# Score rows turned by TensorE, output products first in a step, ELU by one exponential, sixteen mask tiles

## The reference

```
h = max(layernorm(x), 0)
# layer 0
D = |h_i - h_j|                       for every pair of nodes of a graph
s = leaky(batchnorm(D W1 + b1)) W2    one score for each pair, symmetric in i, j
A = softmax(where(adj > 0, s + b2, -9e15))
y = leaky(batchnorm((A h) Wg + bg))
x = x + [h, y] Wt + bt
# layer 1
h = max(layernorm(x), 0); v = h W
a = softmax over i of where(adj > 0, leaky(v_i a1 + v_j a2), -9e15)
out = x + elu(a v)
```

## Time and profile before

| | us |
|---|---|
| median of 3 runs | 1188.4 (1184.73 to 1188.98) |
| the profiled execution, its time | 1189.32 |
| the profiled execution, its span | 1187.5 |
| busy in the span: PE, DVE, ACT, POOL | 1062.9, 1058.1, 994.8, 541.3 |
| mean granted TensorE clock | 0.965 |

### The profile page before, as it was taken

One profiled execution on the slowest core, in us unless ns is written; L12 is line 12 of the kernel. 1 busy time (PEld: TensorE's weight loads), 2 busy tenths in 40 slices (PEclk: granted clock), 3 DMA queues, 4 the chain that ended last, 5 costly groups with the idle time before them and its releaser, 6 DMA issues.

```text
span 1187.5 us, 17527 instructions
## 1 busy us (share of the span) xinstructions
PE 1062.9 (90%) x6376; PEld 463.2 (39%) x6376; DVE 1058.1 (89%) x1418; ACT 994.8 (84%) x1238; POOL 541.3 (46%) x251
## 2 busy tenths in 40 slices
PE   3889999999999999999999599999999999548997
PEld 1333333333333333333333212333333333338886
DVE  6899999999999999999999787999999999435787
ACT  3879999999999899999999599898988989006987
POOL 6466667666666666666667101111122211261331
PEclk9989999999999999999999799999999999758998
DMA  6324343434343334343434789999999998700222
GB/s 165 131 118 177 143 173 146 178 142 164 156 178 142 160 160 177 142 168 152 178 142 188 299 305 358 366 355 360 349 358 350 347 348 296 191 4 12 71 80 72
DMA packets 118005, 237.52 MB, mean 200 GB/s; under 512 B 17568, under 2 KB 65952, under 8 KB 117920
## 3 DMA queue, kind: packets, MB, share of 16 engines
q1 hardware_dynamic: 116336, 235.70, 54.6%
q10 hardware_dynamic: 1584, 0.69, 0.3%
HBM read 126.52 MB, written 109.84 MB: 199 GB/s over the span
## 4 chain that ended last, share of the span: by engine, by line
PE 45%; DVE 32%; ACT 9%; issue 7%; DMA 3%; POOL 2%; SPq 1%; POOLq 0%; DVEq 0%; ACTq 0%
PE psum L708 18%; DVE store L275 12%; PE psum L718 11%; PE psum L722 8%; DVE plain_st L979 4%; ACT store L610 3%; ACT store L556 3%; DVE store L1058 3%; DMA early<-score_rows 2%; PE psum L821 1%; PE psum L680 1%; PE psum L698 1%; PE psum L778 1%; PE psum L855 1%; POOL store L475 1%
## 5 line engine op out<-in xcount | busy, mean ns | idle before, releaser
L708 PE MATMUL psum<-store,w1tt_sb 128*64 128x512 f32 x1792 | 426.0, 605 | 37.4 <-ACT store L556 19.2
L275 POOL TENSOR_TENSOR store<-h_ext 128x2048 f32<-128x2048 f32 (+1 forms) x96 | 386.5, 4028 | 140.9 <-PE psum L708 137.0
L275 DVE TENSOR_TENSOR store<-psum,h_ext 128x2048 f32<-128x2048 f32 x160 | 364.0, 2275 | 0.9 <-ACT h_ext L526 0.9
L556 ACT ACTIVATE store<-store 128x2048 f32<-128x2048 f32 x160 | 305.1, 1929 | 15.2 <-DVE store L275 10.3
L708 PEld LDWEIGHTS psum<-store,w1tt_sb 128*64 128x64 f32 x1792 | 121.7, 137 | 277.5 <-issue 223.5
L610 ACT ACTIVATE store<-store,st 128x1024 f32<-128x1024 f32 x192 | 225.8, 1242 | 1.4 <-DVE st L1045 1.4
L718 PE MATMUL psum<-store,w_twice 128*64 128x512 f32 x768 | 201.5, 603 | 3.9 <-DVE early L944 3.5
L979 DVE BATCH_NORM_STATS2 plain_st<-store 128x6 f32<-128x512 f32 x256 | 160.6, 678 | 0.6 <-ACT store L568 0.6
L722 PE MATMUL psum<-early 128*64 128x512 bf16 x1152 | 158.0, 381 | 0.0
L275 DVE TENSOR_TENSOR store<-h_ext 128x2048 f32<-128x2048 f32 x64 | 139.1, 2173 | 2.6 <-PE psum L708 2.6
L778 PE MATMUL psum<-store,w_rows 128*32 128x512 f32 x1024 | 131.8, 606 | 5.4 <-ACT store L610 5.4
(11 more groups left out here) (153 smaller groups left out, 1143.4 us busy)
## 6 DMA issues: line engine op xcount, KB each, us to landing
kept_products<-store SPq DMA_DIRECT2D x192, 512.0 KB, 2.7
store<-kept_products SPq DMA_DIRECT2D x192, 512.0 KB, 7.5
early<-score_skew SPq DMA_DIRECT2D x16, 384.0 KB, 6.4
early<-adj SPq DMA_DIRECT2D x16, 256.0 KB, 8.0
early<-adj_t SPq DMA_DIRECT2D x16, 256.0 KB, 3.0
store<-x SPq DMA_DIRECT2D x16, 256.0 KB, 4.8
out<-early SPq DMA_DIRECT2D x16, 256.0 KB, 2.4
score_rows<-early SPq DMA_DIRECT2D x64, 32.0 KB, 3.7
```

Of the source, the lines that this page charges most:

```text
L275: return engine.tensor_tensor(t[:, :, 0:steps, :], nodes.unsqueeze(2).broadcast_to([C, 2, steps, N]), windows(h_ext[:, 2 * c, :], STEP * m ...
L556: nc.scalar.activation(t, t, ACT.Abs).then_inc(abs_ready, 1)
L708: last = nc.tensor.matmul(t[MID * g:MID * g + MID, b, :], w1tt_sb[:, 0:MID], diff[slot][:, g, b * BANK:b * BANK + BANK], start=True, stop= ...
```

## The change

1. **Score rows.** The DRAM buffer `score_rows`, `store_rows`, `load_dist` and `s_dist` are gone. PE turns the four 128x128 pieces of `s_rows` directly at `DIST_T`, now 21 and no longer 32, and DVE sorts them into `s_turn` by four smaller operations in place of one. All steps behind move to: TURN 22, SUM 37, SCORES 39, EXP 43, NORM 45, TURN_P 48, COPY 49, MIX 51, MIX_COPY 52, OUT 55, Y 57; STORE_SKEW 24, LOAD_HALF 30, LOAD_ADJ 22.
2. **The half sum.** `att_sum` is four transposes and no longer eight products; the straight half is added to the mask by a new POOL operation behind `sum_half` (`half_masked`), for which `att_scores` waits.
3. **Plain chunk 7.** In pass 2 `subtract` does all eight distances in one operation (`repeats=True`); the doubled half of distance 64 is dropped later by `last_mask`.
4. **POOL in the tail.** All 16 `x_and_bias` stand behind the last quad's `sum_half`; the loads of `x` are issued 6 and 10.
5. **PE in the last stage.** The list is `outputs(t+1)`, `values(t-5)`, `turn2(t-3)`, `dense(t-4)`, `attend(t-6)`.
6. **ELU.** ACT does one exponential of the attended values from PSUM; DVE does min(exp, 1) + the rest.
7. **Masks.** Each of sixteen masks has its own tile; six are made in pass 2 as before, ten at steps 1 to 10 of the last stage, their loads issued before it.

```diff
-        EVAC, DIST_T, TURN, SUM, SCORES, EXP, NORM, TURN_P, COPY, MIX, MIX_COPY, OUT, Y = \
-            19, 32, 33, 50, 52, 56, 58, 61, 62, 64, 65, 67, 69
-        STORE_ROWS, LOAD_DIST, STORE_SKEW, LOAD_HALF, LOAD_ADJ = 21, 26, 35, 41, 30
-        TAIL = 72
+            19, 21, 22, 37, 39, 43, 45, 48, 49, 51, 52, 55, 57
+        STORE_SKEW, LOAD_HALF, LOAD_ADJ = 24, 30, 22
+        TAIL = 60
...
+                pool.wait_ge(half_summed, j + 1)
+                nc.gpsimd.tensor_tensor(mneg[:, :, :], mneg[:, :, :], s_half[:, :, 0:N], ALU.add).then_inc(half_masked, 1)
...
             for j in range(NQ):
                 mask(j)
-                if j == NQ - 1:
-                    pool.wait_ge(bt_ready, 1)
-                    for q in range(8):
-                        x_and_bias(q)
                 sum_half(j)
-                if 5 <= j < 5 + MRING:
+                if 5 <= j < 5 + MADE:
                     mask_l1(j - 5)
-            for q in range(8, NQ):
+            pool.wait_ge(bt_ready, 1)
+            for q in range(NQ):
                 x_and_bias(q)
...
-                nc.scalar.activation(MIN[j % 2], bank(A_BANK[j % 2]), ACT.Relu, scale=-1.0).then_inc(neg_ready, 1)
-                act.wait_ge(neg_ready, j + 1)
-                nc.scalar.activation(MIN[j % 2], MIN[j % 2], ACT.Exp, scale=-1.0).then_inc(neg_exp, 1)
+                nc.scalar.activation(MIN[j % 2], bank(A_BANK[j % 2]), ACT.Exp).then_inc(neg_exp, 1)
...
             def turn_dist(j):
-                pe.wait_ge(dist_in, 16 * (j + 1))
+                pe.wait_ge(rows_ready, j + 1)
                 at_one(QCH * j + DIST_T)
-                for b in range(QUAD):
-                    last = nc.tensor.transpose(att[1].rearrange("p b n -> p (b n)")[:, DIST * b:DIST * b + DIST],
-                                               s_dist[0:DIST, b, :], ident[0:DIST, 0:DIST])
+                for d in range(4):
+                    last = nc.tensor.transpose(att[1][:, d, :], s_rows[:, N * d:N * d + N], ident[:, :])
...
             for t in range(-1, STEPS):
-                for lag, do in ((TURN2, turn2), (DENSE, dense), (MASKED, values), (ATTEND, attend), (-1, outputs)):
+                for lag, do in ((-1, outputs), (MASKED, values), (TURN2, turn2), (DENSE, dense), (ATTEND, attend)):
...
-                nc.vector.tensor_tensor(s_turn[:, :, :],
-                                        att[1].rearrange("p b n -> p (b n)")[:, 0:QUAD * DIST]
-                                        .rearrange("p (b d) -> p b d", b=QUAD),
-                                        last_mask[:, :].unsqueeze(1).broadcast_to([N, QUAD, DIST]), ALU.mult)\
-                  .then_inc(turn_ready, 1)
+                turned_rows = att[1].rearrange("p d (q m) -> p d q m", q=4)
+                in_order = lambda t: t.rearrange("p (r q d) -> p r q d", r=4, q=4)
+                for b in range(QUAD):
+                    last = nc.vector.tensor_tensor(in_order(s_turn[:, b, :]),
+                                                   turned_rows[:, :, :, 4 * b:4 * b + 4].rearrange("p d q r -> p r q d"),
+                                                   in_order(last_mask[:, :]), ALU.mult)
+                last.then_inc(turn_ready, 1)
...
-                nc.vector.tensor_tensor(OUT_T[j % 4], OUT_T[j % 4], MIN[j % 2], ALU.add).then_inc(out_ready, 1)
+                nc.vector.scalar_tensor_tensor(OUT_T[j % 4], MIN[j % 2], 1.0, OUT_T[j % 4], ALU.min, ALU.add)\
+                  .then_inc(out_ready, 1)
```

More of the change, by code:

```diff
@@ L55 @@
 LEAD_DIFF = 7
-MRING = 6
+MADE = 6
 LEAD_PROD = 3
@@ L209, in two_layers @@
         x_in2 = [sem(f"x_in2_{j}") for j in range(NQ)]
-        adjt_in = [sem(f"adjt_in{q}") for q in range(MRING)]
+        adjt_in = [sem(f"adjt_in{j}") for j in range(NQ)]
         out_stored = [sem(f"out_stored{q}") for q in range(4)]
@@ L264, in own, with subtract @@
             return h_ext[:, 2 * c:2 * c + 2, 0:N]
-        def subtract(engine, c, m, slot, op, nodes):
+        def subtract(engine, c, m, slot, op, nodes, repeats=False):
             t = diff[slot].rearrange("p g (d i) -> p g d i", i=N)
             steps = STEP
-            if m == PER - 1:
+            if m == PER - 1 and not repeats:
                 steps = STEP - 1
@@ L301, in two_layers @@
         OUT_T = [by_graph(late(512 * q, 512)) for q in range(4)]
-        MASK = [by_graph(late(5120 + 512 * q, 512)) for q in range(MRING)]
-        adjt = [by_graph(late(5120 + 512 * q, 512).bitcast(I32)) for q in range(MRING)]
+        spare = plain_st[:, :, :, :].rearrange("p n t s -> p (n t s)")
+        mask_at = [late(5120 + 512 * q, 512) for q in range(MADE)] + \
+            [spare[:, 512 * q:512 * q + 512] for q in range(4)] + [late(at, 512) for at in (2560, 3072, 2048, 3584, 4096, 4608)]
+        MASK = [by_graph(t) for t in mask_at]
+        adjt = [by_graph(t.bitcast(I32)) for t in mask_at]
+        TILE_FREE = (mask_ready, s_masked, exp_done, prob_turned, mixed, out_mm)
         O_BANK, T_BANK, D_BANK, W_BANK, A_BANK = (0, 1), 2, 3, (4, 5), (6, 7)
@@ L378, in load_adjt @@
             def load_adjt(j):
-                if j >= MRING:
-                    sp.wait_ge(den_masked, j - MRING + 1)
-                sp.dma_start(adjt[j % MRING], adj_tn[:, quad(j), :]).then_inc(adjt_in[j % MRING], 16)
+                if MADE <= j < NQ - len(TILE_FREE):
+                    sp.wait_ge(pass2_ready, 1)
+                elif j >= MADE:
+                    sp.wait_ge(TILE_FREE[j - NQ + len(TILE_FREE)], NQ)
+                sp.dma_start(adjt[j], adj_tn[:, quad(j), :]).then_inc(adjt_in[j], 16)
             AHEAD = LRING
@@ L393, in _ @@
                           .then_inc(skew_stored[s], 16)
-                for step, do in ((LOAD_ADJ, load_adj), (STORE_ROWS, store_rows), (LOAD_DIST, load_dist),
-                                 (STORE_SKEW, store_skew), (LOAD_HALF, load_half)):
+                for step, do in ((LOAD_ADJ, load_adj), (STORE_SKEW, store_skew), (LOAD_HALF, load_half)):
                     j = quad_at(n - AHEAD, step)
@@ L398, in _ @@
                         do(j)
-                        if step == LOAD_ADJ and 4 <= j < 4 + MRING:
+                        if step == LOAD_ADJ and 4 <= j < 4 + MADE:
                             load_adjt(j - 4)
                         if j == NQ - 1 and step != LOAD_ADJ:
-                            part = (STORE_ROWS, LOAD_DIST, STORE_SKEW, LOAD_HALF).index(step)
-                            for q in range(4 * part, 4 * part + 4):
+                            for q in range(6) if step == STORE_SKEW else range(6, NQ):
                                 load_x(q)
@@ L408, in store_out @@
                 sp.dma_start(out_n[:, quad(j), :], OUT_T[j % 4]).then_inc(out_stored[j % 4], 16)
+            for j in range(MADE, NQ):
+                load_adjt(j)
             for t in range(STEPS + 1):
-                if MRING <= t + 1 < NQ:
-                    load_adjt(t + 1)
                 if 0 <= t - LAST - 1 < NQ:
@@ L805, in att_sum @@
                 for b in range(QUAD):
-                    nc.tensor.matmul(att[0][:, b, :], ident[:, :], s_half[:, b, 0:N], start=True, stop=False)
-                    last = nc.tensor.matmul(att[0][:, b, :], s_half[:, b, 0:N], ident[:, :], start=False, stop=True)
+                    last = nc.tensor.transpose(att[0][:, b, :], s_half[:, b, 0:N], ident[:, :])
                 last.then_inc(s_sum, 1)
@@ L1053, in again @@
                     dve.wait_ge(prod2_ready, p - 1)
-                subtract(nc.vector, c, m, p % 2, ALU.subtract, own(c)).then_inc(abs2_step, 1)
+                subtract(nc.vector, c, m, p % 2, ALU.subtract, own(c), repeats=True).then_inc(abs2_step, 1)
                 dve.wait_ge(abs2_step, p + 1)
@@ L1171, in masked @@
                 for b in range(QUAD):
[L1172 removed]
+                    last = nc.vector.tensor_tensor_reduce(DEN[j % 4][:, b, :], DEN[j % 4][:, b, :], MASK[j][:, b, :],
                                                           -1.0, 3e38, ALU.add, ALU.min, soft[:, j % 4, 0, b:b + 1])
```

39 lines of the change are left out of this document (12 added, 27 removed).

## The result

The changed kernel takes 1216.93 us (median of 4 runs, 1216.54 to 1217.86); beside it the kernel before took 1188.69 (median of 4 runs, 1184.73 to 1195.84). The ratio is 1.0241, with a 95% interval of 1.0212 to 1.0269. The forecast of 1196.4 had the sign right and the size wrong: +28 us where +8 stood, and outside the range.

A forecast was written before the change was run, and what follows sets the result against it. DVE was taken to bound pass 2, and in the last stage PE's attend waiting for DVE's chain, which starts after outputs. Pass 2 +8, tail -16, last stage +16 made +8 on 1188.4: 1196.4 us, range 1183 to 1208.

The forecast's parts named there:

- The loop of the last stage: Last stage: outputs first in PE's list closes a PE-ACT loop, steps 8.09 us against 6.63; stage +16 us (+12 to +18).
- The shorter ELU: Last stage: eight ELUs at the end, each one ACT operation shorter, give -4.5 us; inside the loop it is hidden.
- The clock: Rival, last stage: PE's clock falls in the loop's 2.3 us gaps, 3 to 13 us, taken as 5 (1201); chance 0.17.
- the 2.76 of the row: Last stage, kernel before: a PE gap of 2.76 us ended at the lower clock level, at the turn2 at 1081.02.
- Pass 2: Pass 2, bound by DVE: +0.7 us per quad (0.1 to 1.7) for 12 quads, +8 us (+2 to +14).
- POOL's new addition costs DVE something where they meet: Pass 2: one meeting in two quads, +0.2 us per quad (0 to 0.41), from a subtraction taking 2.42 against 2.01.
- The rest of pass 2: Pass 2, per quad: four sorting operations in place of one, +0.25 us; DVE's wait for PE's turned rows, 0.2 us.
- Chunk 7: Pass 2: one full subtraction in place of memset and two subtractions, +0.02 us, twice, counted as nothing.
- The start of attention: Pass 2: attention starting 13 chunks earlier costs about what the waits for score_rows had cost; counted as nothing.
- The tail: From the last scores' end to the last stage: shorter chain, then POOL's 16 x_and_bias late next; -16 us (-12 to -18).
- Sum: Whole kernel: pass 2 +8, tail -16, last stage +16, together +8 us on 1188.4, giving 1196.4 us.
- list of cases: Forecast as summed 0.45; nothing measurable 0.22; clock falls 0.17; loop stays open 0.10; slow last copy of row layout 0.06.

The follow-up runs named there:

- e1_old_order: The changed kernel with PE's list of the last stage in the old order (outputs last); ratio 0.9964 to the kernel before, last stage 115.2 us.
- e3_filler: The changed kernel with eight more transposes, whose result nobody reads, at the end of PE's last-stage step; 1205.19 us, ratio 1.0152 to the kernel before.
- e6_adj_early: The changed kernel with PE's list turn2, dense, outputs, values, attend and LOAD_ADJ 14 in place of 22; 1170.33 us, ratio 0.9857 to the kernel before.
- e12_adj_split: e6_adj_early with four of the sixteen x_and_bias moved ahead of the last sum_half; 1163.82 us, ratio 0.9803 to the kernel before.
- e5_half_on_pe: The changed kernel with PE's list turn2, dense, outputs, values, attend and the straight half added by PE (eight products), not POOL; ratio 1.0 to the kernel before.

## Why the prediction was right in its sign and wrong in its size

- **The loop of the last stage: right, in place and size.** The step was put at 8.09 us, and it is 8.09 in the trace wherever the clock is full. The wait of each `outputs` for `bn_leaky`, and ACT's for `dense`, are as described. The shorter ELU gives 5.2 us in e1_old_order (4.5 in the sum).
- **The clock: the rival came true, and bigger than its mean.** It had a chance of 0.17, and 5 us in a range of 3 to 13. The argument against it, that 2.3 us of idling is less than the 2.76 of the row, failed: of seven gaps of 2.03 us, five were followed by a fall. Each fall cost 1.63 us (estimate 1.5), 8.1 in all; 16 + 8.1 is 24.1 of the measured 24.9. e3_filler shows it by itself. The failing step is the weighing, by which the sum took the clock at nothing: one row at 2.76 that ends at the lower level says nothing of 2.3. In the kernel before, the longest gap of PE that no fall followed has 1.83 us (ahead of 757.40), and every longer one, from 2.72 us on, has the lower level behind it; 2.3 lies between.
- **Pass 2: the mechanism stood in the sum, mis-sized by a factor of five.** "POOL's new addition costs DVE something where they meet" was taken at +0.2 a quad (0 to 0.41), from a row with a mask beside a subtraction. Over the quads between 767 and 995 us the four absolute values of a quad have a mean of 1498 ns for 1258, +0.96, and the four subtractions 2327 ns, 44 over the mean of the full ones before, +0.18: +1.1. The step that failed is the choice of the nearest row: another POOL operation beside another DVE operation. The second fault is that POOL's mask, which waited for `att_scores` before and for its load after, was not followed to its new place. e6_adj_early gives 8.2 us of it back with one constant.
- **The rest of pass 2.** The four sortings take 0.62 us, and the wait ahead of them 0.15; forecast was 0.25 more than 0.42, and 0.2. (The 0.45 for PE's four transposes was worked out with 2 slots each, which would be 0.9; they took 0.66, and the wait stayed small.) Chunk 7 gave nothing, as said. With +1.1 the items make 1.1 + 0.2 + 0.15 = 1.5 a quad against 1.3 measured (16.1 us in 12 quads). The Trainium skill ("VectorE: DVE Perf Modes", the TRN2 errata section) made an estimated 0.22 us of one sorting operation; its mean duration here is 217 ns, so the trace agrees with the duration, but four queued ones end after 0.62 us and not 0.90, since they overlap.
- **The start of attention: counted at nothing, but +2 to +3 us.** From the first to the third score-row copy it is 41.1 us for 38.1 (40.0 in e1_old_order and e3_filler, which have the same pass 2). Quad 0's steps now stand in the chunks of the first two quads, where DVE is full from then on. That this is the cause is not shown: no run isolates it, and it is read from the copies alone.
- **The tail: right.** -16.8 for -16, and POOL's queue of 16 x 1.28 us was late next, as said. e12_adj_split shows that this queue, and not DVE's chain, set it.
- **Sum.** +19.3 - 16.8 + 24.9 = +27.4. Of the 19 us above the forecast, 8 are the clock and about 11 the meetings of POOL and DVE with the 3 of the early start; these are two causes and not one, which is why no single rival of the list held the time. In the list of cases they excluded each other, and both came.

## What to carry to other kernels

When an engine's in-order list is reordered, follow for one step who waits for whom across both engines: an operation that moves ahead of the one that feeds its own feeder turns slack of a whole step into a closed loop, and the idle gap of PE can then cost its clock as well. An operation given to an idle engine isn't free if it meets the full one: price it by a row with the same pair of operations, or bound it by the whole duration, and place it beside small operations; here one load issued 8 chunks earlier was worth 8 us. When two steps have fixed places in a list, count what the waiting engine does between them and not the steps: two chunks covered PE's eight products before the change and no longer did at the new places (1.44 us a quad in e5_half_on_pe, gone with one step more).

## What the hardware showed that I had not expected

- PE's clock fell after five of seven idle gaps of 2.03 us, but not after one of 2.92; with gaps of 1.16 us in e3_filler it stayed at 1.00 over the window 1120 to 1160. A PE that does more useless work made the kernel faster.
- The meeting of DVE and POOL depends on the pair. DVE's absolute value over 2048 elements (1.23 us alone) took 1.51 beside a POOL mask, 1.64 beside the end of `sum_half`, and 2.18 beside the end of the addition of two inputs. The subtraction at 885.13 that began just ahead of the mask kept its 2.29 us, and POOL paid, with 4.16 for 1.92; the one at 875.98 that began just behind the start of `sum_half` took 2.80.
- Two edits that each gave over 8 us gave 9.5 together: a collision is removed once, whichever side moves.
